# A two-layer gated cross-attention block on one core: the experts of layer one move from inside the attention steps to a stage of their own between the layers

## What is computed

```python
x = x + tanh(g_xattn[0]) * L0_xattn(ctx, layernorm(x), mask)   # 8 heads of 64, keys = ctx rows + tokens
x = x + tanh(g_ffn[0])   * L0_ffn(layernorm(x))                # per token the best 2 of 8 experts
x = x + tanh(g_xattn[1]) * L1_xattn(ctx, layernorm(x), mask)   # 16 heads of 64
x = x + tanh(g_ffn[1])   * L1_ffn(layernorm(x))                # rounded weights, conv over 3 tokens, silu
# one expert e, for the rows routed to it:
y = (silu(h @ w1[e].T) * (h @ w3[e].T)) @ w2[e].T              # 256 -> 512 -> 256
```

## Time and profile before

| | |
|---|---|
| runs | 1511.71, 1522.95, 1533.22 us |
| profiled execution | 1511.2 us, of which the span of its instructions is 1509.4 us |
| busy share of the span | TensorE 84%, GpSimd 74%, VectorE 70%, ScalarE 64% |
| mean granted TensorE clock | 0.945 of full speed |
| DMA | 239.96 MB, mean 159 GB/s |

### The profile page before, as it was taken

One profiled execution on the slowest core, in us unless ns is written; L12 is line 12 of the kernel. 1 busy time (PEld: TensorE's weight loads), 2 busy tenths in 40 slices (PEclk: granted clock), 3 DMA queues, 4 the chain that ended last, 5 costly groups with the idle time before them and its releaser, 6 DMA issues.

```text
span 1509.4 us, 45217 instructions
## 1 busy us (share of the span) xinstructions
PE 1266.7 (84%) x16918; PEld 992.1 (66%) x16918; DVE 1055.9 (70%) x2830; ACT 973.3 (64%) x2319; POOL 1112.8 (74%) x1359
## 2 busy tenths in 40 slices
PE   1777788668879889868999999999999999999952
PEld 1445566447658767646888888677777777776742
DVE  4778788976556556775666666678878778777744
ACT  2678787455446566645656565777778777787831
POOL 5778888696567675457676777788888988888764
PEclk9999999889989999989999999999999999999965
DMA  9599998495998974448999998455455456355520
GB/s 313 138 204 237 252 237 186 75 232 141 249 204 235 230 161 84 95 98 196 240 247 255 251 261 221 93 102 107 92 98 101 100 103 106 87 104 99 79 41 7
DMA packets 438329, 239.96 MB, mean 159 GB/s; under 512 B 388848, under 2 KB 420320, under 8 KB 429024
## 3 DMA queue, kind: packets, MB, share of 16 engines
q1 hardware_dynamic: 408216, 178.51, 57.6%
q10 hardware_dynamic: 26824, 51.22, 11.2%
q0 software_dynamic: 3072, 7.34, 1.8%
HBM read 107.78 MB, written 35.50 MB: 95 GB/s over the span
## 4 chain that ended last, share of the span: by engine, by line
PE 23%; POOL 17%; ACT 16%; DMA 12%; DVE 12%; issue 9%; DVEq 4%; SPq 3%; ACTq 3%; POOLq 0%
POOL probs L649 5%; PE bank_ring L1128 5%; DMA probs_turned<-probs 5%; DMA expert_up<-experts_up 5%; ACT scores L844 4%; PE bank_ring L1090 4%; ACT probs L851 4%; DVE scores L1344 4%; PE bank_ring L1076 3%; PE bank_ring L1143 2%; DMA context<-in_ctx 2%; ACTq L987 2%; ACT keys L864 2%; ACT values L871 2%; PE bank_out L1109 2%
## 5 line engine op out<-in xcount | busy, mean ns | idle before, releaser
L649 POOL TENSOR_TENSOR probs<-scores,probs 112x487 f16<-112x487 f32 x384 | 424.9, 1123 | 207.7 <-ACT probs L851 202.1
L844 ACT ACTIVATE scores<-scores,score_min 112x487 f32<-112x487 f32 x384 | 265.9, 694 | 146.0 <-DVE score_min L1344 144.4
L1361 DVE SCALAR_TENSOR_TENSOR values<-bank_ring,values 128x512 f16<-128x512 f32 x192 | 132.4, 690 | 207.8 <-ACT values L871 207.3
L1344 DVE CUSTOM_DVE_ANT_0 scores<-bank_scores,mask 112x487 f32<-112x487 f32 x384 | 238.2, 657 | 1.8 <-PE bank_scores L1049 1.8
L851 ACT ACTIVATE probs<-scores 112x487 f16<-112x487 f32 x384 | 214.6, 604 | 33.0 <-DMA probs_turned<-probs 17.7
L1090 PE MATMUL bank_ring<-weights,kv_B 128*128 128x128 f16 x3072 | 194.9, 220 | 0.9 <-DVE raw_weights L1639 0.6
L1090 PEld LDWEIGHTS bank_ring<-weights,kv_B 128*128 128x128 f16 x3072 | 183.2, 99 | 11.5 <-DVE raw_weights L1639 0.9
L1109 PE MATMUL bank_out<-values,probs_turned 128*128 128x64 f16 x4608 | 170.4, 194 | 23.3 <-DMA probs_turned<-probs 20.8
L1076 PE MATMUL bank_ring<-kv_B,weights 128*128 128x488 f16 x768 | 181.9, 373 | 9.3 <-DVE keys L1356 9.2
L871 ACT ACTIVATE values<-bank_ring 128x512 f16<-128x512 f32 x192 | 112.2, 584 | 100.4 <-PE bank_out L1109 96.3
L1109 PEld LDWEIGHTS bank_out<-values,probs_turned 128*128 128x128 f16 x4608 | 157.2, 99 | 28.0 <-DMA probs_turned<-probs 14.1
(11 more groups left out here) (230 smaller groups left out, 2479.4 us busy)
## 6 DMA issues: line engine op xcount, KB each, us to landing
expert_up<-experts_up SPq DMA_DIRECT2D x43, 1024.0 KB, 5.3
expert_down<-experts_down SPq DMA_DIRECT2D x43, 512.0 KB, 6.8
raw_weights<-in_weights ACTq DMA_DIRECT2D x8, 1536.0 KB, 11.1
experts_up<-expert_up ACTq DMA_DIRECT2D x8, 1024.0 KB, 5.0
raw_weights<-in_weights ACTq DMA_DIRECT2D x6, 1024.0 KB, 8.9
probs_turned<-probs SPq DMA_TRANSPOSE x384
context_turned_B<-kv_B ACTq DMA_DIRECT2D x16, 375.0 KB, 8.5
kv_B<-context_turned_B ACTq DMA_DIRECT2D x16, 375.0 KB, 3.7
```

The lines of the kernel that those rows point to most:

```text
L649: pool.tensor_tensor(PR[:, u % 4, 1, 0:KEYS], S[:, u % 4, 0:KEYS], PR[:, u % 4, 0, 0:KEYS], ALU.subtract).then_inc(probs_split, 1)
L844: act_e.activation(S[:, u % 4, 0:KEYS], S[:, u % 4, 0:KEYS], ACT.Exp, bias=rmin[:, u % 4:u % 4 + 1], scale=-1.0, accum_out=rsum[:, g % 2, ...
L1344: dve.tensor_tensor_reduce(out=S[:, u % 4, 0:KEYS], in0=bS[u % 2][0:TOK, 0:KEYS], in1=mask[:, m, 0:KEYS], scale=1.0, scalar=3.0e38, op0=AL ...
L1361: dve.scalar_tensor_tensor(vN[:, j % 2, 1].rearrange("p t d -> p (t d)"), bank("v", j)[:], 1 / WSCALE, vN[:, j % 2, 0].rearrange("p t d -> ...
```

## The change

**One expert stage.** Steps are renumbered. Layer one keeps steps 0 to 63. Steps 64 to 119 hold no attention. Layer two starts at step 120 (`B_STEP`). All tokens share one set of slots: routing runs in four groups of sequences (0 to 4, 5 to 9, 10 to 13, 14 and 15) at steps 27, 47, 63 and 70; `place_rows` keeps the room left in each expert's last tile and opens new tiles only for what exceeds it. So 35 tiles hold all rows. Scatters go two a step. The weights of the choice (`weigh_choice`, `weigh_experts`) are computed once for all tokens, at steps 77 to 82. The tiles run in steps 75 to 109, `down` two steps after `up`. Rows come by a plain DMA and are turned by TensorE (`turn_rows`, four transposes) with a ScalarE copy (`copy_rows`). Expert weights have three buffers instead of two; the third lies where layer one's weights were. Both halves of `up` follow each other in the step, as do both gatings on VectorE and both splits on GpSimd.

**Preparations.** One expert chunk a step (steps 1 to 48) instead of two. Rounding the feed-forward's weights moves to steps 52 to 65, splitting layer two's to steps 67 to 82.

**VectorE's order.** Products of late tasks are read in their own step, between `split_k` and `split_v`, instead of behind the next step's masks.

The core of the diff (functions whose bodies only change names are left out, as is the arithmetic of `place_rows`):

```diff
-FIRST_STEP, LAST_STEP = -9, PAIRS + 21
+
+
+GROUPS = ((0, 5), (5, 10), (10, 14), (14, 16))
+TILES = (2 * TOK * NSEQ + EXPERTS * 127) // 128
+SCATTERS = 2
+XR_SLOTS = 8
+ZERO_DMAS = -(-TILES // XR_SLOTS)
+
+
+def slack(g):
+    return 0 if g == NSEQ - 1 else 1
+
+
+def routed(b):
+    n = GROUPS[b][1] - 1
+    return 4 * n + 10 + slack(n)
+
+
+FIRST_TILE = routed(len(GROUPS) - 1) + 5
+DOWN_LAG = 2
+B_STEP = FIRST_TILE + TILES + DOWN_LAG + 8
+FIRST_STEP, LAST_STEP = -9, B_STEP + 8 * NSEQ + 21
 PT_BUFS = 5
 
 
-BATCHES = ((0, 6), (6, 16))
-TILES = tuple((2 * TOK * (b - a) + EXPERTS * 127) // 128 for a, b in BATCHES)
-SCATTERS = (3, 4)
-XR_SLOTS = 10
...
+    if 0 <= s < A_STEPS:
+        return s
+    return s - B_STEP + A_STEPS if B_STEP <= s < B_STEP + PAIRS - A_STEPS else None
...
-WSUM_STEP = 31
-FFN_SUM_STEP, FFN_STEP = 26, 32
-L1_STEP = 41
+FFN_SUM_STEP, WSUM_STEP, FFN_STEP = 52, 57, 58
+L1_STEP = FFN_STEP + 9
+WEIGH_STEP = FIRST_TILE + 2
 
 
 def expert_chunks(j):
-    i = 2 * (j - EXPERT_STEP)
-    return range(i, i + 2) if 0 <= i < EXPERTS * MOE_CHUNKS else range(0)
+    i = j - EXPERT_STEP
+    return range(i, i + 1) if 0 <= i < EXPERTS * MOE_CHUNKS else range(0)
...
-            def load_rows(b, i):
-                t = tile(b, i)
-                if i == 0:
-                    sp.wait_ge(scattered[b], 16 * len(scatters(b)))
+            def load_rows(t):
+                if t == 0:
+                    for b in range(len(GROUPS)):
+                        sp.wait_ge(scattered[b], 16 * len(scatters(b)))
                 if t >= 2:
-                    sp.wait_ge(up_ready, 2 * (t - 2) + 2)
-                sp.dma_start_transpose(xT[:, t % 2], xs[b][128 * i:128 * i + 128, :])\
-                    .then_inc(xt_loaded[t % 2], 16)
-
-            def load_expert(b, i, part):
-                t = tile(b, i)
-                if i == 0 and part == 0:
-                    sp.wait_ge(slots_ready, b + 1)
+                    sp.wait_ge(rows_turned, t - 1)
+                sp.dma_start(rows_in[:, t % 2], xs[128 * t:128 * t + 128, :]).then_inc(rows_loaded[t % 2], 16)
+
+            def load_up(t):
+                if t == 0:
+                    sp.wait_ge(slots_ready, len(GROUPS))
                     sp.wait_ge(ex_stored[0], 32 * 4)
                     sp.wait_ge(ex_stored[1], 32 * 4)
-                e = sp.value_load(ids[b][0:1, i:i + 1], min_val=0, max_val=EXPERTS - 1)
-                if part == 0:
-                    if t >= 2:
-                        sp.wait_ge(up_ready, 2 * (t - 2) + 2)
-                    sp.dma_start(eup[:, t % 2], up_dram[e]).then_inc(up_loaded[t % 2], 16)
-                else:
-                    if t >= 2:
-                        sp.wait_ge(down_ready, t - 1)
-                    sp.dma_start(edown[:, t % 2], down_dram[e]).then_inc(down_loaded[t % 2], 16)
-
-            def store_result(b, i):
-                t = tile(b, i)
+                e = sp.value_load(ids[0:1, t:t + 1], min_val=0, max_val=EXPERTS - 1)
+                if t == 2:
+                    sp.wait_ge(v_ready, A_STEPS)
+                if t >= 3:
+                    sp.wait_ge(up_ready, 2 * (t - 3) + 2)
+                sp.dma_start(tile_ups[t % 3], up_dram[e]).then_inc(up_loaded[t % 3], 16)
...
+                if j == FIRST_TILE - 2:
+                    load_up(0)
+                    load_down(0)
+                    load_rows(0)
+                    load_rows(1)
+                    for t in (1, 2):
+                        load_up(t)
+                        load_down(t)
+                i = tile_up(j)
+                if i is not None:
+                    if i + 2 < TILES:
+                        load_rows(i + 2)
+                    if i + 3 < TILES:
+                        load_up(i + 3)
+                if 2 <= j - FIRST_TILE and j - FIRST_TILE + 1 < TILES:
+                    load_down(j - FIRST_TILE + 1)
+                if tile_down(j) is not None:
+                    store_result(tile_down(j))
...
-                if m[0]:
-                    round_hidden(m[0][1], m[0][2], m[0][3])
+                    round_k(pair(j + 2))
+                if tile_up(j) is not None:
+                    round_hidden(tile_up(j), 0)
+                if tile_turn(j) is not None:
+                    copy_rows(tile_turn(j))
+                if tile_up(j) is not None:
+                    round_hidden(tile_up(j), 1)
...
-                if j == A_STEPS - 2:
+                if j == B_STEP - 2:
                     pe.wait_ge(l1_split, L1_CHUNKS)
                     pe.wait_ge(ffn_rounded, 8)
                 if is_pair(j):
-                    scores(j)
+                    scores(pair(j))
                 if is_pair(j + 2):
-                    layer, n = layer_of(j + 2), seq_of(j + 2)
-                    if j + 2 == 0:
+                    p = pair(j + 2)
+                    layer, n = layer_of(p), seq_of(p)
+                    if p == 0:
                         pe.wait_ge(l0_split, 4)
-                    if j + 2 in (4 * n, start_b(n)):
+                    if p in (4 * n, first_pair_b(n)):
                         pe.wait_ge(kv_ready[layer], n + 1)
                         if layer:
                             pe.wait_ge(kvb_loaded[n % 2], 16 * (n // 2 + 1))
-                    proj_q(j + 2)
-                    proj_k(j + 2)
-                m = micro(j)
-                expert(m[0])
+                    proj_q(p)
+                    proj_k(p)
+                if tile_up(j) is not None:
+                    up(tile_up(j), 0)
+                if tile_turn(j) is not None:
+                    turn_rows(tile_turn(j))
                 for t in early(j):
                     part(t)
                 if is_pair(j):
-                    proj_v(j)
-                expert(m[1])
+                    proj_v(pair(j))
+                if tile_up(j) is not None:
+                    up(tile_up(j), 1)
+                if tile_down(j) is not None:
+                    down(tile_down(j))
                 if is_pair(j - 2):
-                    sum_values(j - 2)
+                    sum_values(pair(j - 2))
                 for t in late(j):
                     part(t)
-                expert(m[2])
...
             for j in STEPS:
-                m = micro(j)
                 if is_pair(j):
-                    mask_scores(2 * j)
-                    mask_scores(2 * j + 1)
-                if is_pair(j + 1) and not halves_in_step(j - 1):
-                    split_k(j + 1)
+                    mask_scores(2 * pair(j))
+                    mask_scores(2 * pair(j) + 1)
                 for g in range(PAIRS // 4):
-                    if slack(g) and j == 4 * g + 6:
+                    if slack(g) and j == group_step(g) + 6:
                         norm_out(g)
-                for t in late(j - 1):
-                    part(t)
                 if is_pair(j + 2):
-                    split_q(j + 2)
-                if is_pair(j - 1) and not halves_in_step(j - 1):
-                    split_v(j - 1)
+                    split_q(pair(j + 2))
                 for n in range(NSEQ):
                     if j == p_step(n, -8, -9):
                         p_apply(n)
...
                 quantise_ffn_weights(j)
                 for c in l1_chunk(j - 1):
                     split_l1_chunk(c)
-                if m[0]:
-                    gate_hidden(m[0][1], m[0][2], m[0][3])
+                if tile_up(j) is not None:
+                    gate_hidden(tile_up(j), 0)
+                    gate_hidden(tile_up(j), 1)
                 for t in early(j):
                     part(t)
                 for n in range(NSEQ):
...
                         stats("M", n)
                     if j == 4 * n + 8 + slack(n):
                         m_apply(n)
-                for b in range(2):
+                for b in range(len(GROUPS)):
                     if j in (routed(b), routed(b) + 1):
-                        choose_experts(b, j - routed(b))
+                        choose_slots(b, j - routed(b))
                     if j == routed(b) + 2:
                         place_rows(b)
-                    if j == routed(b) + 3:
-                        weigh_experts(b)
-                if halves_in_step(j) and is_pair(j + 2):
-                    split_k(j + 2)
+                if j in (WEIGH_STEP, WEIGH_STEP + 2):
+                    weigh_choice((j - WEIGH_STEP) // 2)
+                if j == WEIGH_STEP + 5:
+                    weigh_experts()
+                if is_pair(j + 2):
+                    split_k(pair(j + 2))
+                for t in late(j):
+                    part(t)
                 for g in range(PAIRS // 4):
-                    if not slack(g) and j == 4 * g + 5:
+                    if not slack(g) and j == group_step(g) + 5:
                         norm_out(g)
-                if halves_in_step(j):
-                    split_v(j)
-                if m[2]:
-                    gate_hidden(m[2][1], m[2][2], m[2][3])
```

(43 more changed lines are left out.)

410 lines of the change are left out of this document (209 added, 201 removed).

## The result

The changed kernel took 1573.1 us (median of four runs, 1570.5 to 1577.7) where the kernel before took 1528.1: a ratio of 1.0335, 95% interval 1.0239 to 1.0430. It is **slower by 3%**, outside the range and on the side that was given 18%. The profiled span is 1572.0 us; the forecast span was 1498.

| stretch | forecast | measured |
|---|---|---|
| to step 0 | 50.6 | 49.2 |
| layer one, to step 63 | 427.5 | 459.5 |
| entry, to the first `up` | 54 | 53.9 |
| 35 tiles | 169 | 197.1 |
| exit, to the first mask of layer two | 29 | 25.8 |

What follows compares the result with a forecast made beforehand. Layer one was taken as bound by latency, layer two by TensorE. Terms of 50.6, 427.5, 54, 169, 29, 705 and 62.9 us gave a span of 1498, 1511 on the median's scale; predicted 1503, range 1452 to 1560.

Steps and rivals of the forecast that it cites:

- the side that was given 18%: Whole kernel: a time slower by over 2%, from 1553.4 us on, chance 0.18.
- So a tile costs between 4.4 and 7.5. I take 4.8: Expert stage of 35 tiles: 4.8 us a tile, with 6 for last `up` and slow start, 169 us in all.
- Half the DMA traffic of the weights per step [...] I take 0.2: Layer one: halved weight traffic takes 0.2 us off each step of 7.15, one of three cuts leading to 6.5.
- The routing's 18 us: Layer one: 10 us for 20 added scatters on GpSimd and 8 us for VectorE's three routings.
- I take off both waits whole: 11.6 us in 72 steps, 20 in 127: Layer two: reading late products earlier ends TensorE's waits at `f_max` and `f_rate`, leaving 705 us of 725.
- the cover named for the price: Layer two: VectorE's new wait for TensorE's late task fits in `split_v`'s wait for ScalarE, 0.83 us a step.
- Entry 54: From layer one's last mask at step 63 to the first tile: 54 us, bounds 44 and 62.
- exit 29: From the last `up` to layer two's first mask: 29 us, bounds 24 and 35.
- end 62.9: After layer two's last mask: 62.9 us, the same tasks in the same order.
- Slow feeding: Rival, expert stage: TensorE waits for expert weights at each `up`, 7.5 us a tile, +92 us, 1595; chance 0.08.
- The lower clock: Rival, expert stage: TensorE at 1.2 instead of 2.4 GHz, 8.7 us a tile, +133 us, 1636; chance 0.05.
- The relief doesn't arrive: Rival: layer one stays at 7.15 a step (+41, 1544), TensorE waits elsewhere in layer two (+20, 1523), both 1564; chance 0.17.

Runs made afterwards that it cites:

- three repairs: The changed kernel with rows loaded from ScalarE's queue, raw expert weights three steps after the stores, tile numbers at the end of memory: 1504.8 us, ratio 0.9940.

## Why the prediction was wrong

- *"So a tile costs between 4.4 and 7.5. I take 4.8"* failed, by 28 us: a tile took 5.6, inside the bounds. TensorE's 4.4 was right, and so was the bandwidth: 407 GB/s over the whole stage, once the rows came early. What was missing is a price for the row load. The prediction named the very wait that delays it (`load_up` of tile t+3 for `up` of t), but only as a delay of weights, and not of the rows that stand behind them in SyncE's queue; its "three buffers keep two tiles of loads in flight" is true of the weights alone. The rows had two buffers and a place behind that wait: 4.5 us of lead against 6.4 to land; even the 4.4 of a store of this size in the kernel before leaves nothing. A sum of the lead per load, in place of a mean of bytes, could have shown it. The Trainium skill (DMA: Bandwidth & Descriptors, Where 436 GB/s comes from) puts the limit of one core's HBM traffic at some 358 GB/s, half of what it gives for two cores. The stage without waits moved 402 to 407 on the one core that runs here, so the trace differs again.
- *"Half the DMA traffic of the weights per step [...] I take 0.2"* failed, by about 27 us. The mean did fall (share 0.74 for 0.90). The bursts did not: still 3 MB at a time, and behind three of them, where the context traffic followed two steps later, the turning DMAs stalled; with half of each burst moved three steps the stalls went. Why the kernel before, with bursts of the same size in the same places, has no such steps stays open.
- *The routing's 18 us* were too few. Each routing holds up three steps by 15 to 16 us in all (10.5, 10.0 and 12.9 with three repairs, against 5.9), and two of the three that were counted stand in layer one, beside the scatters. The steps were better than forecast in return: with three repairs 429.8 us, against 427.5, two routings included. That this term comes out is luck.
- *"I take off both waits whole: 11.6 us in 72 steps, 20 in 127"* failed: the order saves 3.6 to 5.9 us over layer two, little more than its traces differ by. The 11.6 also left out a second line of `f_max`, shown below; both waits were 16.7 us in the 72 steps. The waits at `f_rate` went and those at `f_max` halved. But the cover named for the price, `split_v` waiting for ScalarE, is gone in the steps where the chain to `f_rate` is read, as the prediction's price of the move said; in most others it held. Of layer two's excess this is 14 to 16 us; the 32 bytes are 6, which no view of the old trace could show, though the length of the table did. Together that is 2 to 4 more than the excess: with the old order and the addresses of before layer two takes 720.3 us, where the sum began at 725.

```profile
PE bank_ring L1238 <- DVE context L1580: 5.1, 8, 1.1
```

- *Entry 54, exit 29, end 62.9*: right. That VectorE's work makes the entry is shown for 3.3 us of it, by which it fell when the rounding was moved out; the rest is not shown.
- *The rivals.* Slow feeding came, at other loads and at 5.6 us in place of 7.5. The lower clock came with it, for some tiles: 0.94 granted in the stage, and after 2.49 us of waiting an `up` of 2.03 us, where one at 2.4 GHz takes 1.34. It did not go on for 35 tiles. The Trainium skill's rule quoted then (TensorE: Matmul & The Clock Gate, HAM oscillation — how this bites in real kernels) is about loops whose compute per tile is shorter than their wait for data; here a tile has 4.4 us of matmuls and the longest wait was 3.9, so no run shows whether it holds. "The relief doesn't arrive" gave 1523 to 1564. Its second half, that TensorE let go at `f_max` waits for the next thing, is much of what layer two did: it came out 18.5 over the forecast, where this rival had 20. Its first half is not: with three repairs a step of layer one, the two routings taken off, is 6.3 us, where it had 7.15.
- With the three repairs the span is 1497.6, almost the forecast 1498, but that is luck and not its reasons: the stage is 12.5 shorter than forecast and layer two 14.5 longer.

## What to carry to other kernels

For each load in an in-order queue, write down when its issue is allowed and when its data is needed; compare that lead with the landing time under load, not with bandwidth. Bulk traffic beside latency-bound DMAs is to be judged by what is issued close together, not by its mean. When a buffer changes its size, look at where the ones behind it come to lie.

## What the runs showed of the hardware

- 32 bytes of shift of the probabilities and their neighbours took the slowest tenth of the turning DMAs' packets from 18 ns or more to 31 or more, and made the kernel before 0.5% slower (0.2 to 0.9).
- One core moved 402 to 407 GB/s for 155 us with plain DMAs; a 128 KB load landed in 7.0 to 8.3 us meanwhile, and in 2.1 where the first two were issued in an idle stretch.
- DMA engines can be busy and slow: 16 us at a share of 1.18 moved 113 GB/s. Between 110 and 118 us the turning DMAs' 256-byte packets took 188 to 508 ns in the mean of each two microseconds, where 18 are usual.
